# ScalarE takes the first convolution tap of the first three batches, and the second batch's rows pass ahead of a turn

## The reference

```
x = x + attn(layernorm(x))          # this change lies in here
x = x + xattn(layernorm(x), ctx)    # mLSTM cell over q, k, v
x = x + ffn(layernorm(x))           # FP4-quantised gated feed-forward

# attn: a mamba mixer and a gated MLP
zxbcdt = x @ in_proj_w.T                       # z (512), xBC (640), dt (8)
xBC = silu(causal_depthwise_conv(xBC, conv_w, 4 taps) + conv_b)
xs, Bm, Cm = split(xBC)                        # 8 heads x 64, and two of 64 states
dt = softplus(dt_raw + dt_bias); dA = exp(-dt * exp(A_log))
h = h * dA_t + outer(dtx_t, B_t); y_t = h @ C_t      # scan over 256 positions
y = rms((y + D * xs) * silu(z)) @ out_proj_w.T
x = x + y; x = x + (a * silu(g)) @ fc2_w.T           # a, g = rms(x) @ fc1_w.T
```

## Time and profile before

| | |
|---|---|
| median of 3 runs | 619.11 us (616.53 to 620.52) |
| profiled execution | 616.92 us, its span 615.2 us |
| TensorE busy | 568.1 us (92%), 2991 products |
| VectorE busy | 440.9 us (72%) |
| ScalarE busy | 270.2 us (44%) |
| GpSimd busy | 145.5 us (24%) |
| mean granted TensorE clock | 0.961 |
| line 1092, later taps on VectorE | 120 instructions, 50.8 us |
| line 1082, first taps on VectorE | 30 instructions, median 348 ns |
| line 898, first taps on ScalarE | 10 instructions, median 508 ns |

### The profile page before, as it was taken

How to read it: one execution, slowest core, us unless ns; L and a number is a source line. 1 busy time by engine, 2 the same in 40 slices (tenths; PEclk the granted TensorE clock), 3 DMA queues, 4 the chain that set the end, 5 groups by cost and what they waited for, 6 DMA issues and landing times. The chain is left out here.

```text
span 615.2 us, 9562 instructions
## 1 busy us (share of the span) xinstructions
PE 568.1 (92%) x2991; PEld 463.6 (75%) x2991; DVE 440.9 (72%) x963; ACT 270.2 (44%) x564; POOL 145.5 (24%) x209
## 2 busy tenths in 40 slices
PE   6989999989999899999999997699957899999995
PEld 5767666878888788888888887588844577777774
DVE  6985896398986144454455446558898999999994
ACT  3667778776794432221111112444512444444431
POOL 4130000253543310201101101005665222122200
PEclk9999999799999999999999999779967899999998
DMA  8301011000000500000000000324400000000000
GB/s 294 121 2 34 18 35 39 4 23 6 6 3 2 209 1 2 1 0 1 0 2 1 0 1 0 107 58 133 121 1 0 1 18 17 9 17 17 18 18 27
DMA packets 22528, 20.99 MB, mean 34 GB/s; under 512 B 12120, under 2 KB 20696, under 8 KB 22104
## 3 DMA queue, kind: packets, MB, share of 16 engines
q1 hardware_dynamic: 22008, 20.41, 10.2%
q10 hardware_dynamic: 480, 0.07, 0.1%
HBM read 16.04 MB, written 2.34 MB: 30 GB/s over the span
## 5 line engine op out<-in xcount | busy, mean ns | idle before, releaser
L778 PE MATMUL ps<-xnT,w_fc 128*128 128x256 f32 x512 | 112.8, 380 | 0.0
L778 PEld LDWEIGHTS ps<-xnT,w_fc 128*128 128x128 f32 x512 | 96.5, 190 | 12.7
L1565 PE MATMUL ps<-w_fc,scores 128*128 128x352 f32 x256 | 82.6, 477 | 5.9 <-ACT scores L1631 5.9
L1565 PEld LDWEIGHTS ps<-w_fc,scores 128*128 128x128 f32 x256 | 49.1, 197 | 33.1 <-ACT scores L1631 7.1
L1190 DVE TENSOR_TENSOR xs<-ps,xs 128x512 f32<-128x512 f32 x32 | 22.1, 692 | 60.8 <-ACT xs L996 60.8
L996 ACT ACTIVATE xs<-ps 128x512 f32<-128x512 f32 x32 | 19.1, 597 | 95.8 <-PE ps L778 75.7
L791 PE MATMUL ps<-zs,xs 128*128 128x256 f32 x256 | 56.6, 379 | 0.0
L791 PEld LDWEIGHTS ps<-zs,xs 128*128 128x128 f32 x256 | 48.6, 190 | 6.6
L1092 DVE SCALAR_TENSOR_TENSOR fold<-xpad,conv_w,fold 128x256 f32<-128x256 f32 x120 | 50.8, 481 | 2.4 <-ACT fold L898 1.6
L1583 PE MATMUL ps<-u_res,hT 128*128 128x256 f32 x192 | 45.9, 391 | 3.8 <-DVE scores L1737 2.8
L1583 PEld LDWEIGHTS ps<-u_res,hT 128*128 128x128 f32 x192 | 37.3, 195 | 11.7 <-issue 3.0
(11 more groups left out here) (263 smaller groups left out, 1176.7 us busy)
## 6 DMA issues: line engine op xcount, KB each, us to landing
zs<-in_ffn_w SPq DMA_DIRECT2D x1, 2112.0 KB, 10.7
x_res<-in_x SPq DMA_DIRECT2D x8, 256.0 KB, 7.7
w_fc<-in_w_fc SPq DMA_DIRECT2D x1, 2048.0 KB, 10.3
xnT<-in_ctxT SPq DMA_DIRECT2D x8, 256.0 KB, 3.1
xs<-in_ctxT SPq DMA_DIRECT2D x8, 256.0 KB, 3.3
xs<-xnT SPq DMA_DIRECT2D x8, 256.0 KB, 3.4
xs<-in_ctx SPq DMA_DIRECT2D x16, 128.0 KB, 2.6
out<-scores SPq DMA_DIRECT2D x16, 128.0 KB, 1.7
```

The costliest lines, as they stand in the source:

```text
L778: last = pe.matmul(bank[half + r][:, i * S:(i + 1) * S], m.w_fc1[:, kk, col:col + P], m.xnT[:, b, kk * S:(kk + 1) * S], start=(kk == 0), s ...
L1565: last = pe.matmul(bank[1 + j][:, 0:HALF], xT[:, p, k * P:(k + 1) * P], m.w_gu[:, k, j * HALF:(j + 1) * HALF], start=(k == 0), stop=(k == ...
```

## The change

It does three things. The set of batches whose first tap ScalarE takes becomes 0, 1 and 2; it was 6 and 7. `rows` of batch 1 are issued, both, ahead of `turn_u(6)` in step 4, as those of batch 0 are ahead of `turn_u(4)` in step 3. And the counts that VectorE waits for are worked out by functions over the set, since batches with two own steps (of `conv_step`) now come before those with three. ScalarE's wait for `silu_ready` is left out where its value would not be positive.

```diff
-    TAPPED = 6
+    TAPPED = (0, 1, 2)
+    ROWS_FIRST = (3, 4)
+    conv_steps = lambda b: sum(NCH * (PAD - 1 if i in TAPPED else PAD) for i in range(b))
+    taps_before = lambda b: NCH * sum(1 for i in TAPPED if i < b)
...
                 on(channels, k - 2, [0, 1, 2])
-                if k == 3:
-                    rows(0, 0)
-                    rows(0, 1)
+                if k in ROWS_FIRST:
+                    rows(k - 3, 0)
+                    rows(k - 3, 1)
                 on(turn_u, 2 * k - 2)
-                if k > 3:
+                if k not in ROWS_FIRST:
                     on(rows, k - 3, 0)
                 on(channels, k - 2, [3, 4])
...
-                if k > 3:
+                if k not in ROWS_FIRST:
                     on(rows, k - 3, 1)
...
         def first_tap(b, k):
             n, ch = NCH * b + k, ORDER[k]
             act.wait_ge(s["xpad_ready"], n + 1)
-            act.wait_ge(s["silu_ready"], NCH * (b - 1))
+            after(act, s["silu_ready"], NCH * (b - 1))
...
-                on(first_tap, k - 2 if k - 2 >= TAPPED else B, i)
+                on(first_tap, k - 2 if k - 2 in TAPPED else B, i)
...
-                    if tap == 0 and b >= TAPPED:
+                    if tap == 0 and b in TAPPED:
                         dve.wait_ge(s["xpad_ready"], n + 1)
-                        dve.wait_ge(s["tap_ready"], n + 1 - NCH * TAPPED)
+                        dve.wait_ge(s["tap_ready"], taps_before(b) + k + 1)
                         continue
...
-                    if b < TAPPED:
-                        before = PAD * (NCH * b + tiles[0]) + len(tiles) * (tap - 1) + (k - tiles[0]) + 1
-                    else:
-                        before = (PAD * NCH * TAPPED + (PAD - 1) * (NCH * (b - TAPPED) + tiles[0])
-                                  + len(tiles) * (tap - 2) + (k - tiles[0]) + 1)
-                    if b < TAPPED or tap > 1:
-                        dve.wait_ge(s["conv_step"], before)
+                    own = PAD - 1 if b in TAPPED else PAD
+                    done = tap - 1 if b in TAPPED else tap
+                    if done:
+                        dve.wait_ge(s["conv_step"], conv_steps(b) + own * tiles[0] + len(tiles) * (done - 1)
+                                    + (k - tiles[0]) + 1)
```

## The result

| | kernel before | changed kernel |
|---|---|---|
| median | 620.30 us (20 runs, 616.53 to 623.29) | 616.15 us (20 runs, 613.97 to 622.39) |
| ratio of changed to before | | 0.9939, interval 0.9920 to 0.9957 |
| profiled execution, its span | 616.92 us, 615.2 us | 615.06 us, 613.3 us |
| mean granted clock in it | 0.961 | 0.958 |

The change makes the kernel 0.6% faster, 3.8 us by the ratio (2.7 to 5.0 by its interval); forecast were 3.7 us and a median of 615.4, from a median before of 619.11. The two profiled executions differ by only 1.9 us, 615.06 where 613.2 was forecast. What is missing there is weights that landed 0.69 us later and 1.3 us of half clock on TensorE, and most of the experiments' surprises are TensorE's clock too.

The account below looks back on a forecast made before the run. VectorE was taken as full in the early steps, TensorE in the later part. Gains of 0.24 + 1.82 + 0.37 + 1.23 = 3.7 us turn a median of 619.11 us into 615.4, range 610.6 to 619.4.

Parts of the forecast that it names:

- step 3: Early step of the first function: `turn_u(4)` starts 0.82 us earlier, taps in ScalarE's chain eat 0.58; gain 0.24 us.
- step 4: Next early step: TensorE's wait before `turn_u(6)` goes and the second `rows` no longer stands behind `turn_x(1, 0)`; gain 1.82 us.
- step 8: Late step where ScalarE took taps before: without them `turn_x` starts at 87.32 instead of 87.69; gain 0.37 us.
- step 9: Late step: all of TensorE's 1.23 us idling before `turn_x` goes, as 2.1 us of taps leave ScalarE.
- VectorE's bound in step 8: VectorE ends the last three products of batch 5 only at 86.78, limiting the gain there to 0.37 us.
- its cover at the begin of the scan: VectorE's idle time ahead of a product at 105.98 hides the 2.9 us of taps given back, 0.2 us left.
- the 2.43: TensorE's idling in us before `turn_u(6)` in the kernel before, forecast gone with VectorE 2 x 1.44 us earlier.
- The rule: Advice to multiply on VectorE and not on ScalarE; by it the early batches would lose from the moved taps.
- Rival A: TensorE's half clock at 110 to 116 us moves: gone, 613.4 us (chance 0.12); once more, 617.4 us (0.06).
- B: Ten taps given back delay VectorE in steps 8 and 9, which then gain nothing: 617.0 us; chance 0.13.
- C: ScalarE, served in order, is the late engine in steps 2 to 4: 3.8 us of loss, 622.9 us; chance 0.04.
- D: Nothing changes, the early part being covered by a later fixed point: 619.1 us; chance 0.07.

## Why the prediction was right

| term | forecast | measured |
|---|---|---|
| step 3 | 0.24 | 0.38 |
| step 4 | 1.82 | 2.05 |
| step 8 | 0.37 | 0.32 |
| step 9 | 1.23 | 1.21 |
| sum | 3.66 | 3.96 |

**The sum** held in every term, and the timing (3.8 us) with it. That they meet within 0.1 us is luck, since the timing's interval is more than 1 us to each side. The median of 616.15 lies 0.75 us above the forecast mainly because the one before, over 20 runs, lies 1.2 us above that of the three. Steps 3 and 4 came out 0.14 and 0.23 us better mostly for one reason: I put `turn_u` at the end of the last product of `rows` (6.27 us behind the step's begin), but the next instruction starts 0.16 us before that end, at 6.11 and 6.03. The chain from `turn_u` to `turn_x` was forecast at 4.24 and is 4.20.

**VectorE's bound in step 8** and **its cover at the begin of the scan** stood as forecast: 0.77 us of waiting for the fifth tile, and 0.19 us to spare against 0.2. The test with no taps showed both again, without the early part.

**Which part gains.** The steps were right, but I read rows 1 too readily as "VectorE is full, so relief pays". My own step 4 held the answer: VectorE has its rows ready at 5.2 us into the step, and with the moved rows nobody asks before 6.0. So once the rows are moved, the 2.43 go without VectorE being 2 x 1.44 us earlier. The runs split the early 2.4 us: moved rows alone 2.7 at full clock, taps alone 0.4 + 1.7, both together 2.4. They are two cures for one wait, and the taps of batches 1 and 2 cost 0.6 us of ScalarE's chain in steps 3 and 4 each. Batch 0's relief is the one that pays, by the length of step 3, since `rows` already stand ahead of `turn_u(4)`.

**The rule** of the Trainium skill, "ScalarE: Activation LUTs", Rules for kernel authors, on multiplying on VectorE was set aside for the early batches. In sum it did better than I did: late, taking the taps off ScalarE gained 1.5 us; early, only batch 0's five are worth having there (12.32 and 12.24 against 12.98 and 12.89), and only by the step lengths.

**Rival A** was right in kind. It happened upwards in the profiled execution (1.32 us, forecast 2.0, for a second fall), and the 20 runs of each kernel seem to even it out. The prediction had it as one fall that might move; it is a matter of several places, and the one behind the context's products never went away while they were narrow. Two executions of one program had their first fall 58 us apart, which agrees with what I cited from the Trainium skill, "TensorE: Matmul & The Clock Gate", What's actually happening, that the window runs free of the kernel's start. **B**, **C** and **D** did not happen: the first by the scan's product, the second as TensorE idled 0.44 and not 2 us, the third as the rest is 497.5 and 497.6 us.

## What to carry to other kernels

Before relieving a full engine, look whether the one that waits for it has other work that could stand ahead; here, in the early steps, reordering two groups of products did what fifteen moved multiplications did, and both together did no more. Then count what the relief lengthens on the other engine's chain, per batch, and keep only the part that nothing else can give. When two profiles are compared, compare the lengths of steps, with the granted clock beside each: a late load moved the steps of single executions by 0.7 us and falls of the clock by 1 to 5 us, as much as the change.

## What the runs showed of the hardware

Short runs of narrow products can cost more than their own time. Behind 16 to 32 products of 8 columns, TensorE's granted clock fell from full to half, 1.2 GHz, and the products behind them took 1.5 to 1.9 times as long (`rows` 2.91, 3.18, 3.63 us for 1.94; twelve products of `channels` 5.17 for 2.75). Behind the context's 24 and 32 it fell in all twelve profiles, though not at the same one of the two. Behind the 16 of `time_steps` it fell in six of twelve.

With 48 and 64 columns in the context's products, in about the same time, the clock stayed full there in both profiles taken, and with 32 in those of `time_steps` (1.87 us for 1.85) in both too. The two together brought the median from 616.15 to 612.08 us, the ratio from 0.9939 to 0.9860, at the same step lengths. Their executions lie between 611.1 and 613.7 us, the changed kernel's between 614.0 and 622.4, but these are 5 against 27, and a range grows with the number. A kernel that used these idle columns with its real data was not tried.

TensorE's idling of 1.2 to 2.4 us in the kernel before was followed by no fall in its profile. The fall at 11 us in two runs came behind waits of 0.84 us for ScalarE and 0.92 and 1.05 us for the weights' load. The other twelve profiles, without a fall there, wait 0.84 us for ScalarE too, but 0.72 us at most for the load. Whether that is the cause was not tested.
